# The first layer's edge stage, written out item by item in place of engine loops of twelve items

## What is computed

```python
q = (feat @ Wq.T + bq).reshape(n, H, HD)          # H = 8 heads of HD = 32
k = (feat @ Wk.T + bk).reshape(n, H, HD)
v = (feat @ Wv.T + bv).reshape(n, H, HD)
score = jnp.einsum('ehd,ehd->eh', q[edge_dst], k[edge_src])
score = jnp.clip(score / math.sqrt(HD), -10.0, 10.0)
...
ex = jnp.exp(score - smax[edge_dst])
den = jax.ops.segment_sum(ex, edge_dst, num_segments=n)
alpha = ex / den[edge_dst]
wv = jax.ops.segment_sum(alpha[:, :, None] * v[edge_src], edge_dst, num_segments=n).reshape(n, C)
```

## Time and profile before

| | |
|---|---|
| median of three timed runs | 4422.83 us |
| the profiled execution: span from first to last instruction | 4980.9 us |
| mean granted TensorE clock in it | 0.851 |
| edge stage: first and last gather start | 144.0 and 889.0 us |
| edge stage: last addition starts | 912.3 us |

### The profile page before, as it was taken

The page is one execution under the profiler, slowest core; times in us unless marked ns, Lnnn a source line. Parts: engine busy times, 40 slices in busy tenths (PEclk is TensorE's granted clock), DMA queues, the critical chain, the costliest instruction groups (busy, mean ns, idle before and its releaser), DMA issues. The chain is left out here.

```text
span 4980.9 us, 76392 instructions
## 1 busy us (share of the span) xinstructions
PE 3649.6 (73%) x19614; PEld 2886.2 (58%) x19615; DVE 2794.6 (56%) x8633; ACT 2014.6 (40%) x6637; POOL 2027.2 (41%) x2092
## 2 busy tenths in 40 slices
PE   6677777795999457778778678776726665667995
PEld 3455555585888346666545566665624444456885
DVE  4567676646122457776666677765726555773112
ACT  0466666421222137668633567665310100021221
POOL 0566665000222025666611466663066666202221
PEclk9788887896999769999988799998856676778998
DMA  2566666354778657776633677664344443304556
GB/s 77 180 185 183 188 181 178 93 151 105 259 266 279 229 212 224 213 222 204 180 114 138 205 214 242 207 178 137 118 154 146 140 127 106 93 27 155 190 179 222
DMA packets 353521, 859.19 MB, mean 172 GB/s; under 512 B 52389, under 2 KB 162828, under 8 KB 344588
## 3 DMA queue, kind: packets, MB, share of 16 engines
q0 software_dynamic: 144384, 455.22, 30.5%
q1 hardware_dynamic: 208780, 399.80, 24.3%
HBM read 770.02 MB, written 84.81 MB: 172 GB/s over the span
## 5 line engine op out<-in xcount | busy, mean ns | idle before, releaser
L1866 POOL DMA_INDIRECT h<-h_table,src_of x944 | 907.2, 961 | 1050.0 <-PE ps L1900 505.5
L1880 PE MATMUL ps<-h,gat_layer_hot 128*128 128x261 f32 (+1 forms) x3136 | 896.6, 436 | 302.0 <-issue 93.3
L1880 PEld LDWEIGHTS ps<-h,gat_layer_hot 128*128 128x128 f32 x3136 | 636.9, 213 | 475.8 <-issue 260.4
L745 POOL DMA_INDIRECT edges_rows<-kv_table,src_of x464 | 462.0, 996 | 402.5 <-DVE edges_out_rows L844 150.6
L2138 DVE TENSOR_TENSOR acc<-acc,ps 128x522 f32 (+1 forms) x696 | 418.0, 601 | 308.9 <-PE ps L1880 168.2
L1965 ACT ACTIVATE h<-h,gat_shared 128x128 f32<-128x128 f32 x1872 | 581.1, 390 | 4.6 <-issue 2.5
L1866 POOL DMA_INDIRECT x<-h_table,src_of x448 | 429.8, 959 | 227.9 <-issue 111.5
L1880 PE MATMUL ps<-x,gat_layer_hot 128*128 128x261 f32 (+1 forms) x1504 | 425.5, 432 | 114.2 <-DVE x L2115 47.0
L1032 ACT ACTIVATE acc<-ps,moe_experts_b 128x256 f32<-128x256 f32 (+1 forms) x512 | 200.5, 443 | 614.2 <-PE ps L982 590.7
L1880 PEld LDWEIGHTS ps<-x,gat_layer_hot 128*128 128x128 f32 x1504 | 303.2, 211 | 195.2 <-issue 95.1
L982 PE MATMUL ps<-moe_experts_turned,moe_experts_w 128*128 128x256 f32 (+1 forms) x2048 | 403.3, 355 | 5.0 <-DMA moe_experts_w<-in_L_ffn_W 5.0
(11 more groups left out here) (377 smaller groups left out, 5693.7 us busy)
## 6 DMA issues: line engine op xcount, KB each, us to landing
moe_experts_w<-in_L_ffn_W SPq DMA_DIRECT2D x128, 1024.0 KB
gat_layer_hots<-hot_table SPq DMA_DIRECT2D x174, 562.0 KB
hot_table<-acc SPq DMA_DIRECT2D x58, 562.0 KB
h<-h_table,src_of POOLq DMA_INDIRECT x944
edges_dst_row<-dst_rows SPq DMA_DIRECT2D x58, 256.0 KB
acc<-src_rows SPq DMA_DIRECT2D x58, 256.0 KB
acc<-dst_rows SPq DMA_DIRECT2D x58, 256.0 KB
h_table<-h SPq DMA_DIRECT2D x10, 1280.0 KB
```

Source lines behind the costliest of these rows:

```text
L745: nc.gpsimd.indirect_dma_start(rows[:, r, s, :], None, k.kv_table, bass.IndirectOffsetOnAxis(ap=k.src_of[:, 2 * t + s:2 * t + s + 1], axis ...
L1866: nc.gpsimd.indirect_dma_start(g.rows(t, e, 0, W), None, g.table, bass.IndirectOffsetOnAxis(ap=k.src_of[:, 2 * t + e:2 * t + e + 1], axis= ...
L1880: mm = nc.tensor.matmul(k.ps[t % S * PIECES + p][:, 0:PIECE], hot[:, t % HOTS, e, :], g.rows(t, e, p * PIECE, (p + 1) * PIECE), start=(e = ...
```

## The change

`ringed` goes, and `written` takes its place: the same steps in the same order, but for all 232 items in plain code, with no loop. The four engines that had loops (PE, DVE, ACT, SP) have none now. Every number of an item is a constant, so waits compare with constants, the raised semaphores are gone, and a wait that can't be short for the first items is left out there. Four waits that another wait implies are gone: PE's for `exped` ahead of the sums, DVE's for `weighted` ahead of the addition, DVE's for `cleared` in all additions but the first, and ACT's for the row of destinations in three items of four. POOL's code only loses the 4 that were added to its count.

```diff
-def ringed(eng, n, ring, steps):
+def written(n, steps):
 
     depth = len(steps) - 1
-    steps = [s if s else (lambda t, r, i: None) for s in steps]
-
-    def turn(base, i, r, limit):
+    for r in range(-depth, n):
         for j, step in enumerate(steps):
-            d = r + depth - j
-            if d >= 0 and d < limit:
-                step(base + d, d % ring, i + d // ring)
-
-    for r in range(-depth, 0):
-        turn(0, 0, r, n)
-    whole = n // ring - 1
-    with eng.Fori(0, whole) as i:
-        for r in range(ring):
-            turn(i * ring, i, r, n)
-    for r in range(n - whole * ring):
-        turn(whole * ring, whole, r, n - whole * ring)
+            if step and 0 <= r + depth - j < n:
+                step(r + depth - j)
...
         def _(sp):
-            def load(b, slot):
-                sp.dma_start(dst_row[:, slot, :], item_rows(k.dst_rows, 4 * b, 4)).then_inc(row_in[slot], 16)
-
-            for slot in range(BATCHES):
-                load(slot, slot)
-            turns, over = divmod(ITEMS // 4 - BATCHES, BATCHES)
-            with sp.Fori(0, turns) as i:
-                for slot in range(BATCHES):
-                    sp.wait_ge(hot_t_made, i * RING + (4 * slot + 4 + SH))
-                    load(i * BATCHES + (BATCHES + slot), slot)
-            for slot in range(over):
-                sp.wait_ge(hot_t_made, turns * RING + 4 * slot + 4 + SH)
-                load(turns * BATCHES + BATCHES + slot, slot)
+            for b in range(ITEMS // 4):
+                if b >= BATCHES:
+                    sp.wait_ge(hot_t_made, 4 * (b - BATCHES) + 4)
+                sp.dma_start(dst_row[:, b % BATCHES, :], item_rows(k.dst_rows, 4 * b, 4)).then_inc(row_in[b % BATCHES], 16)
...
                 if t >= RING:
-                    pool.wait_ge(weighted, S + t - RING + 1)
+                    pool.wait_ge(weighted, t - RING + 1)
...
-            act.sem_inc(hot_t_made, SH)
-            act.sem_inc(exped, S)
-            act.sem_inc(hot_made, S)
-
-            def one_hot_t(t, r, i):
-                act.wait_ge(row_in[r // 4], (i + 1) * 16)
-                act.wait_ge(q_made, free(t))
-                act.activation(hot_t[:, r % SH, :], dst_row[:, r // 4, r % 4 * 256:(r % 4 + 1) * 256], ACT.Abs,
+            def one_hot_t(t):
+                if t % 4 == 0:
+                    act.wait_ge(row_in[t // 4 % BATCHES], (t // RING + 1) * 16)
+                if t >= SH:
+                    act.wait_ge(q_made, t - SH + 1)
+                act.activation(hot_t[:, t % SH, :], dst_row[:, t // 4 % BATCHES, t % 4 * 256:(t % 4 + 1) * 256], ACT.Abs,
                                bias=minus_p[:, 0:1]).then_inc(link_a, 1)
                 act.wait_ge(link_a, t + 1)
-                act.activation(hot_t[:, r % SH, :], hot_t[:, r % SH, :], ACT.Relu, bias=one_col[:, 0:1], scale=-1.0
+                act.activation(hot_t[:, t % SH, :], hot_t[:, t % SH, :], ACT.Relu, bias=one_col[:, 0:1], scale=-1.0
                                ).then_inc(hot_t_made, 1)
 
-            def exps(t, r, i):
-                act.wait_ge(clipped, ready(t, S))
-                act.wait_ge(summed, free(t))
-                act.activation(out_rows[:, r % S, :, C:W], score[:, r % S, :].rearrange("p (s h) -> p s h", s=2),
...
-            ringed(act, ITEMS, RING, [one_hot_t, None, None, None, None, None, exps_and_one_hot])
+            written(ITEMS, [one_hot_t, None, None, None, None, None, exps_and_one_hot])
...
-            pe.sem_inc(q_made, SH)
-            pe.sem_inc(summed, S)
-
-            def q_of_edges(t, r, i):
-                n = pe.value_load(k.item_tile[0:1, bass.ds(t, 1)], min_val=0, max_val=TILES - 1)
-                pe.wait_ge(hot_t_made, ready(t, SH))
-                pe.wait_ge(multiplied, free(t))
+            def q_of_edges(t):
+                n = pe.value_load(k.item_tile[0:1, t:t + 1], min_val=0, max_val=TILES - 1)
+                pe.wait_ge(hot_t_made, t + 1)
+                if t >= S:
+                    pe.wait_ge(multiplied, t - S + 1)
                 for s in range(2):
-                    mm = nc.tensor.matmul(psq[r % S][:, s * C:(s + 1) * C], hot_t[:, r % SH, s * P:(s + 1) * P],
+                    mm = nc.tensor.matmul(psq[t % S][:, s * C:(s + 1) * C], hot_t[:, t % SH, s * P:(s + 1) * P],
                                           row(k.h, n, 0, C), start=True, stop=True)
                 mm.then_inc(q_made, 1)
 
-            def sums(t, r, i):
-                pe.wait_ge(weighted, ready(t, S))
-                pe.wait_ge(exped, ready(t, S))
-                pe.wait_ge(hot_made, ready(t, S))
-                pe.wait_ge(added, free(t))
+            def sums(t):
+                pe.wait_ge(weighted, t + 1)
+                pe.wait_ge(hot_made, t + 1)
+                if t >= S:
+                    pe.wait_ge(added, t - S + 1)
                 for s in range(2):
-                    mm = nc.tensor.matmul(pso[r % S][:, 0:W], hot[:, r % S, s * P:(s + 1) * P], out_rows[:, r % S, s, :],
+                    mm = nc.tensor.matmul(pso[t % S][:, 0:W], hot[:, t % S, s * P:(s + 1) * P], out_rows[:, t % S, s, :],
                                           start=(s == 0), stop=(s == 1))
                 mm.then_inc(summed, 1)
 
-            ringed(pe, ITEMS, RING, [q_of_edges] + [None] * 6 + [sums])
+            written(ITEMS, [q_of_edges] + [None] * 6 + [sums])
...
-            for s in (multiplied, reduced, clipped, weighted, added):
-                dve.sem_inc(s, S)
-
-            def multiply(t, r, i):
-                dve.wait_ge(gathered[r], (i + 1) * 32)
-                dve.wait_ge(q_made, ready(t, SH))
-                dve.wait_ge(reduced, t + S - 1)
-                v.tensor_tensor(prod[:, r % 2], psq[r % S][:, 0:2 * C].rearrange("p (s c) -> p s c", s=2), rows[:, r, :, 0:C], ALU.mult
+
+            def multiply(t):
+                dve.wait_ge(gathered[t % RING], (t // RING + 1) * 32)
+                dve.wait_ge(q_made, t + 1)
+                if t >= 2:
+                    dve.wait_ge(reduced, t - 1)
+                v.tensor_tensor(prod[:, t % 2], psq[t % S][:, 0:2 * C].rearrange("p (s c) -> p s c", s=2), rows[:, t % RING, :, 0:C], ALU.mult
                                 ).then_inc(multiplied, 1)
 
...
-            def add(t, r, i):
-                n = dve.value_load(k.item_tile[0:1, bass.ds(t, 1)], min_val=0, max_val=TILES - 1)
-                dve.wait_ge(weighted, ready(t, S))
-                dve.wait_ge(summed, ready(t, S))
-                dve.wait_ge(cleared, 1)
-                dve.wait_ge(added, t + S)
-                v.tensor_tensor(row(k.acc, n, 0, W), row(k.acc, n, 0, W), pso[r % S][:, 0:W], ALU.add
+            def add(t):
+                if t == 0:
+                    dve.wait_ge(cleared, 1)
+                n = dve.value_load(k.item_tile[0:1, t:t + 1], min_val=0, max_val=TILES - 1)
+                dve.wait_ge(summed, t + 1)
+                if t:
+                    dve.wait_ge(added, t)
+                v.tensor_tensor(row(k.acc, n, 0, W), row(k.acc, n, 0, W), pso[t % S][:, 0:W], ALU.add
                                 ).then_inc(added, 1)
 
-            ringed(dve, ITEMS, RING, [multiply, reduce, clip, None, weigh, None, None, add])
+            written(ITEMS, [multiply, reduce, clip, None, weigh, None, None, add])
```

More of the change, by code:

```diff
@@ L761, in one_hot_t, with exps @@
                                bias=minus_p[:, 0:1]).then_inc(link_a, 1)
                 act.wait_ge(link_a, t + 1)
-                act.activation(hot_t[:, r % SH, :], hot_t[:, r % SH, :], ACT.Relu, bias=one_col[:, 0:1], scale=-1.0
+                act.activation(hot_t[:, t % SH, :], hot_t[:, t % SH, :], ACT.Relu, bias=one_col[:, 0:1], scale=-1.0
                                ).then_inc(hot_t_made, 1)
-            def exps(t, r, i):
-                act.wait_ge(clipped, ready(t, S))
-                act.wait_ge(summed, free(t))
-                act.activation(out_rows[:, r % S, :, C:W], score[:, r % S, :].rearrange("p (s h) -> p s h", s=2),
+            def exps(t):
+                act.wait_ge(clipped, t + 1)
+                if t >= S:
+                    act.wait_ge(summed, t - S + 1)
+                act.activation(out_rows[:, t % S, :, C:W], score[:, t % S, :].rearrange("p (s h) -> p s h", s=2),
@@ L770, in exps, with one_hot @@
                                ACT.Exp).then_inc(exped, 1)
-            def one_hot(t, r, i):
+            def one_hot(t):
                 for s in range(2):
-                    last = act.activation(hot[:, r % S, s * P:(s + 1) * P], k.iota_row[:, 0:P], ACT.Abs,
-                                          bias=k.dst_in[:, bass.ds(2 * t + s, 1)], scale=-1.0)
+                    last = act.activation(hot[:, t % S, s * P:(s + 1) * P], k.iota_row[:, 0:P], ACT.Abs,
+                                          bias=k.dst_in[:, 2 * t + s:2 * t + s + 1], scale=-1.0)
@@ L776, in one_hot, with exps_and_one_hot @@
                 last.then_inc(link_h, 1)
                 act.wait_ge(link_h, t + 1)
```

(40 more changed lines are left out.)

## The result

The changed kernel takes 4432.09 us (median of 20 runs, 4426.74 to 4437.57), the kernel before 4424.60 us in the same rounds (20 runs, 4419.21 to 4430.69). The ratio is 1.0018, 95% interval 1.0012 to 1.0024: the change costs some 7.5 us. I forecast a gain of 2.

What follows compares the result with a forecast made beforehand. GpSimd's gathers were taken to pace the edge stage at 612 us, VectorE having 99 us of slack. The terms summed to 0 to -3 us for timed runs, so 4422.83 - 2 = 4421 us, range 4395 to 4445 (own range 4410 to 4430).

Steps and rivals of the forecast that it cites:

- The bound: Edge stage: GpSimd's gathers pace it in timed runs, 612 us for 232 items, against VectorE's 513 us.
- The pauses: Edge stage: VectorE's idle times, taken as profiler writing; profiled span falls 134 to 151 us, timed runs 0.
- B: Edge stage: pauses are the program's own, from register waits in loops, and go; about 4283 us; chance 0.12.
- C: Edge stage: pauses are the program's own, hang on the register load that stays; 4420 us; chance 0.08.
- 1: Loop control of the edge stage: 2.4 us an engine, beside VectorE's and GpSimd's work, so 0.
- 3: Waits left out in the edge stage: each is implied by one that stays, so 0.
- 4: Raised semaphores: a dozen instructions ahead of the edge stage, during the first gather; below 1 us.
- Term 5: Written-out code of the edge stage: some 61 more blocks read, 26 us inside VectorE's 99 us slack, so 0.
- Rival D: Edge stage: written-out code isn't fetched in time; slower, 4432 to 4449 us, 4441 in the middle; chance 0.10.
- Term 2: Register arithmetic of the edge stage's waits: at most 46 us of VectorE's sequencer, covered, so 0.
- my own sign of being wrong: Timed median outside 4410 to 4430 us would mean the pauses or GpSimd's pace were misread.
- the sum for GpSimd: Edge stage: 464 gathers of 996 ns, 462.0 us, plus gaps 144.5 us and clearing 5.6 us, give 612 us.

Runs made afterwards that it cites:

- 2: Kernel before with items written out on all four engines, every wait, raised semaphore and register load kept: 4430.74 us, ratio 1.0015.
- 9: Kernel before with the items of TensorE alone written out: 4423.38 us, ratio 1.0005.
- 11: Kernel before with the items of ScalarE alone written out: 4423.64 us, ratio 1.0003.
- 13: Changed kernel with VectorE's wait for rows put last of the multiplication's three waits, two idle increments behind it: 4424.10 us, ratio 1.0004.
- 7: Kernel before, looped, with the weighing's second operand in PSUM and a VectorE copy added: 4406.26 us, ratio 0.9963.
- 8: Changed kernel, written out, with the weighing's second operand in PSUM and a VectorE copy added: 4404.09 us, ratio 0.9958.
- 6: Kernel before with 128 idle increments behind each load in SyncE's engine loop, which stays a loop: 4423.14 us, ratio 1.0004.
- 5: Kernel before with SyncE's loop alone written out and 128 idle increments behind each of its 54 loads: 4423.07 us, ratio 1.0004.
- 1: Kernel before, run and recorded again without any edit: 4424.2 us, ratio 1.0004, profiled span 4420.7 us.

## Why the prediction was wrong

*The bound* was right: GpSimd paces the stage in the clean traces. I had 612 us; the clean traces have 747.0 + 1.0 - 143.7 = 604 us before the change and 610 after.

*The pauses* were rightly kept out of the timed runs, and rivals B and C are out. That writing the profile down caused them was my estimate from the earlier trace rows, and no run shows it. They belonged to that one recorded execution and were not confined to this stage, so that the span fell to 4430 us and not to 4840.

*Terms 1, 3 and 4* came out as put, as far as the runs can tell: with all waits kept the time is the changed kernel's (2), and TensorE and ScalarE written out cost nothing (9, 11).

*Term 5, code,* was 0 as put. Reads by the two instruction queues in the changed kernel, from 144 to 760 us:

```profile
q8 instruction: 20, 0.33, 0.2%
q14 instruction: 41, 0.34, 0.2%
```

That is 61 against 12 in before (the 9 of the earlier trace rows and 3 of the other queue, which I had left out), so 49 more where I had 61. Rival D's mechanism is absent, and that the time lies at the lower end of its range, and inside the range that I had widened for it, is luck: VectorE's addition has 1.5 us of idle time, and a kernel that reads about as many blocks (13: 20 and 45) is at 1.0004.

*Term 2, register arithmetic, is the step that failed*: "if that cover went GpSimd still covers 612 - 513 = 99 us: 0". It measured +7 us. I asked only whether the arithmetic delayed VectorE, and took its removal as harmless at worst. Where VectorE waits for rows it is the distance between the rows' arrival and the multiplication, and by that between the next weighing and the gathers. By my own sign of being wrong (a median outside 4410 to 4430 us) it was the pace of GpSimd that was misread.

Behind it stands the second error, in the sum for GpSimd: 464 x 0.996 us was taken as a property of the gather, equal in both kernels. The earlier trace rows had 940/947/1513: a mean 50 ns above the median is a tail of 23 us, and I did not ask what made it. Had I asked, its cause would have been found in the trace of before (all 57 of its long gathers meet a weighing), and a change of VectorE's moments would have been a rival of either sign on the pacing engine.

## What to carry to other kernels

On the engine that sets the pace, compare mean with median for each group: a tail of long instructions is time that another engine's instructions may decide; here 0.16 us earlier (0.02 against 0.18 us after the rows) came with 5.7 us more of it. An edit that only takes work off an engine with slack still changes when its next instructions start; ask what they will then coincide with. Where GpSimd gathers beside VectorE, an operand in PSUM in place of a second one in SBUF was worth 0.4% here, even with a copy added.

## What the runs showed of the hardware

- A GpSimd gather that starts at least 0.05 us into a VectorE weighing with two SBUF operands, of which at least 0.13 us is left, is held (74 of 74 in the changed kernel, 38 of 38 in before): it ends 0.82 us after the weighing's end. With one of the two operands in PSUM, 114 and 104 gathers that start in the same way take at most 0.952 us (7, 8). A gather does not hold a weighing for its whole length: 156 weighings that start 0.1 us or more inside a gather take 0.675 to 0.687 us in the changed kernel.
- An engine loop of SyncE with three loads and 384 increments in its body was read anew in every turn (6): 5 to 7 blocks of 8 KB from one branch to the next, 88 more than before over 18 turns, and more than the 55 of the same work written out (5). The kernel before, whose four loops turn 18 times as well, reads 12 blocks from 144 to 760 us (1).
- Two recordings of one program can differ by 560 us (4980.9 and 4420.7) while its timed runs agree within 0.4%.
